# Folding the convolution taps of half the channels into TensorE products of the input projection

## The chip, the cores and the metric

The kernel runs on one core of a Trainium2 chip. The core has five engines that run their own instruction streams and meet only at semaphores: TensorE (PE, with its weight loads PEld), VectorE (DVE), ScalarE (ACT), GpSimd (POOL) and the queue that issues DMAs (SP). The metric is the device time of one execution in microseconds (us); lower is better.

## The reference

Two blocks are applied to x of shape (8, 256, 256): 8 batches, 256 time steps, 256 channels. The first is a gated state space block (Mamba), the second a linear attention with feed-forward. The change is in the front of the first, so only that is shown here:

```python
xn = _layernorm(x, ln_g, ln_b)
xn = xn * (1.0 + scale[:, None, :]) + shift[:, None, :]
xz = jnp.einsum('bsd,ed->bse', xn, in_proj_w)          # (8, 256, 1024)
x_in, z = jnp.split(xz, 2, axis=-1)                    # 512 channels each
xt = jnp.transpose(x_in, (0, 2, 1))
u = jax.lax.conv_general_dilated(xt, conv_w[:, None, :], (1,), [(D_CONV - 1, 0)],
        feature_group_count=DI, ...) + conv_b[None, :, None]   # causal, 4 taps a channel
u = jax.nn.silu(jnp.transpose(u, (0, 2, 1)))
x_dbl = jnp.einsum('bsd,ed->bse', u, x_proj_w)
dt_r, B, C = jnp.split(x_dbl, [DT_RANK, DT_RANK + N], axis=-1)
dt = jax.nn.softplus(jnp.einsum('bsr,dr->bsd', dt_r, dt_proj_w) + dt_proj_b)
# scan over time: h = h * exp(dt * A) + dt * u * B ;  y = sum over n of h * C
y = (y + u * D_param) * jax.nn.silu(z)
x = x + gate[:, None, :] * jnp.einsum('bsd,ed->bse', y, out_proj_w)
```

The convolution is depthwise: each channel d has its own four weights, and output t of channel d is the bias plus w3 x(t) + w2 x(t-1) + w1 x(t-2) + w0 x(t-3).

## The kernel before

The 512 inner channels are four blocks (`dc`) of 128 partitions. The scan over 16 states of a block is cut into four units of 4 states by 256 steps, so a batch is 16 units and the whole kernel 128 units. A unit g = 16 b + i goes through the engines like this: POOL makes the driving terms dt·u·B (line 530, `hs`, ten buffers); ACT makes the decays exp(dt·A), four activations (line 722, `ring`, two PSUM buffers); DVE scans (line 950) and multiplies by C (line 957); in four units of sixteen (i = 1, 5, 9, 13) POOL does that multiplication instead (line 539); PE sums the states by transposing adds into `sums` (lines 1293 and 1298). DVE gates a finished block with silu(z) (line 964, `ygT`).

All other work is hung into this stream at fixed places. Each engine's program is one loop over g, and tables of slots say at which g a step is issued; a step at slot -16 of batch b is issued with unit i = 0 of batch b - 1, one at slot -14 with i = 2, one at slot 19 of batch b with i = 3 of batch b + 1. So while batch b - 1 is scanned, the input projection of batch b and the attention of batch b - 2 are done between its units. Each engine works strictly through its own list.

The part that the change touches is the input projection of batch b (`in_proj`) and its convolution:

- PE, `in_proj(b, 0)` and `in_proj(b, 1)` (line 1242): two blocks of x each, four products of 128x128 weights with 256 columns. From batch 2 on all four parts of the projection use one PSUM bank, `PX`, so each has to wait until the one before has been read. `in_proj(b, 2)` and `in_proj(b, 3)` (line 1247) are z.
- ACT, `conv_last_tap(b, h)` (line 615): reads half h out of PSUM, scaled by the last tap, plus the bias, into `conv`.
- DVE, `conv_taps(b, h)` (line 916): six multiply-adds, three taps of two blocks, each reading the PSUM bank again, shifted by the tap, and adding to `conv`.
- ACT, `silu_u(b)`, then `x_proj` and `dt_proj` on PE, and so on to the next batch's decays.

Around it stand, on PE, `q_times_att` (line 1428) and `sum_states`; behind it `transpose_back` (line 1316) and `out_proj` (line 1350) of the batch before; on ACT, `decays` of unit i = 2 ahead of `conv_last_tap(b, 1)` and those of i = 3 behind it. Batch 1 is placed otherwise: both halves of x are projected in the prologue, before unit 0, into `PX` and `PY`, ahead of `setup_emb` (lines 1204 and 1187).

Of the kernel before, what the change touches and what calls it, by code (L numbers as in the profile page):

```python
# [19 lines left out]
P = 128  # L20
# [16 lines left out]
THIRDS = (0, 64, 96)  # L37
SPLIT = THIRDS[-1] + 1
ONES_ROW = RANK + 2 * N
LAST_B = NB - 1  # L40
NROW = (4 * D + NB * T) // P

# [60 lines left out]
    return None if b == 1 else b  # L103


def build(nc, a, out):
    ctx = ExitStack()
    with ctx:
        def sb(name, shape):
            return ctx.enter_context(nc.sbuf_tensor(name, shape, F32))  # L110
# [7 lines left out]
        def sem(name):  # L118
            return ctx.enter_context(nc.semaphore(name))
# [32 lines left out]
        zs = sb("zs", [P, 2, TC, DI])  # L152
        xdbl = sb("xdbl", [ONES_ROW + 1, T])
        conv = sb("conv", [P, DC, T])
        vln = conv
        dt, dtu = sb("dt", [P, 2, DC, T]), sb("dtu", [P, 2, DC, T])

# [31 lines left out]
        PZ = ps("PZ", [P, 2, T])  # L189


        staged = hs[:, 5:10].rearrange("p s n t -> p (s n t)")
        adaT = staged[:, 0:3 * KC * D].rearrange("p (k s e) -> p k s e", k=KC, s=3)
        embT = staged[:, 3 * KC * D:5 * KC * D].rearrange("p (k s e) -> p k s e", k=KC, s=2)
# [7 lines left out]
        s_ld_win = sem("ld_win")  # L202
        s_ld_w = sem("ld_w")
        s_ld_post = sem("ld_post")
        s_pool_const = sem("pool_const")
        s_sc_ready = sem("sc_ready")
        s_aexp_ready = sem("aexp_ready")
# [107 lines left out]
        def pcol(name, lo=0, hi=None):  # L315
            s, e = COLS[name]
            return par[:, s + lo:(e if hi is None else s + hi)]
# [39 lines left out]
        def _(sp):  # L357
# [23 lines left out]
            def broadcast_bc(b):  # L381

                sp.wait_ge(s_xdbl_ready, b + 1)
                sp.dma_start(bc_dram[b % 2], xdbl[RANK:RANK + 2 * N, :]).then_inc(s_bc_stored, 16)
                sp.wait_ge(s_bc_stored, 16 * (b + 1))
                if b == 0:
                    broadcast_b(b, 0)
                    for q in range(1, UPC):
                        broadcast_b(b, q)
                        broadcast_c(b, q - 1)  # L390
                    broadcast_c(b, UPC - 1)
                else:
                    for q in range(UPC):
                        broadcast_b(b, q)
                    for q in range(UPC):
                        broadcast_c(b, q)
# [11 lines left out]
            def load_seg(tile, src, seg, n, sem):  # L408
                sp.dma_start(tile, src[:, seg:seg + n].rearrange("(k p) e -> p k e", p=P)).then_inc(sem, 16)
# [14 lines left out]
            load_seg(adaT[:, :, 2], a["ada_wT"], 2 * D, D, s_ld_emb)  # L424
            load_seg(embT[:, :, 0], a["W_emb"], 0, D, s_ld_emb)
            load_seg(embT[:, :, 1], a["W_emb"], D, D, s_ld_emb)
            broadcast_bc(0)
            sp.dma_start(wo[:, :, :], a["out_wT"].rearrange("(k p) e -> p k e", p=P)).then_inc(s_ld_post, 16)
            for i, w in enumerate(("Wq", "Wk", "Wv", "W_out")):
# [33 lines left out]
        def _(pool):  # L463
# [87 lines left out]
            def rstd2(b):  # L551
                if b >= 1:
                    pool.wait_ge(s_yh_ready, TC * b)
                rstd(s_st2_ready, b, mv2, ve2, rs2, nb2, s_ve2_ready, s_rs2_ready, s_nbp2)

            for g in range(FIRST, LAST):
                if 0 <= g < NB * U:
                    inputs_of(g // U, g % U)
                if 0 <= g - BEHIND < NB * U and by_pool(g - BEHIND):
                    states_times_c((g - BEHIND) // U, (g - BEHIND) % U)  # L560
                for slot, step in ((-17, rstd0), (-1, softplus_0), (3, softplus_1), (26, residual), (28, rstd1),
                                   (40, rstd2)):
                    b = due(g, slot)
                    if b is not None and not (b == LAST_B and slot > 20) and not (b == LAST_B - 1 and step is rstd2):
                        step(b)
# [17 lines left out]
        def _(act):  # L583
# [25 lines left out]
            def conv_last_tap(b, h):  # L609
                act.wait_ge(s_xz_mm, 4 * b + h + 1)  # L610
                if b >= 1:
                    act.wait_ge(s_dt_sum, 2 * b - 1 + h)
                for e in range(2):
                    dc = 2 * h + e
                    nc.scalar.activation(conv[:, dc, :], xz_bank(b, h)[:, e, :], ACT.Identity, bias=pcol("conv_b", dc, dc + 1),  # L615
                                         scale=pcol("conv_w", TAPS * dc + 3, TAPS * dc + 4)).then_inc(s_conv0_ready, 1)

            def copy_z(b):
                if b == 0:
# [22 lines left out]
                nc.scalar.activation(u[:, 0, half], conv[:, half], ACT.Silu).then_inc((s_u_first, s_u_ready)[h], 1)  # L642

            def silu_u(b):
                act.wait_ge(s_tap_done, 3 * DC * (b + 1))
                if b >= 2:
                    act.wait_ge(s_uD_ready, DC * (b - 1))
                nc.scalar.activation(u[:, b % 2], conv[:, :, :], ACT.Silu).then_inc(s_u_ready, 1)
# [242 lines left out]
        def _(dve):  # L891
# [13 lines left out]
                stats(b, xg[:, b % XBUF], st0, mv0, s_st0_ready)  # L905

            def conv_taps(b, h):

                dve.wait_ge(s_conv0_ready, DC * b + 2 * h + 2)
                for s in range(1, TAPS):  # L910
                    for e in range(2):
                        dc = 2 * h + e
                        if s > 1:
                            dve.wait_ge(s_tap_done, 3 * DC * b + 6 * h + 2 * (s - 2) + e + 1)
                        w = pcol("conv_w", TAPS * dc + 3 - s, TAPS * dc + 4 - s)
                        V.scalar_tensor_tensor(conv[:, dc, s:], xz_bank(b, h)[:, e, 0:T - s], w, conv[:, dc, s:], ALU.mult,  # L916
                                               ALU.add).then_inc(s_tap_done, 1)
# [248 lines left out]
        def _(pe):  # L1166
# [42 lines left out]
            def transpose_x(b):  # L1209
# [7 lines left out]
                if b == 0:  # L1217
                    keep_on(8)

            def in_proj(b, h):  # L1220

                if h == 0:
                    pe.wait_ge(s_xn_ready, KD * (b + 1))
                if b == 0:
                    if h == 0:
                        pe.wait_ge(s_ld_win, 16)
                    if h == 2:
                        pe.wait_ge(s_ld_win2, 16)
                elif h == 0:
                    pass  # L1230
                elif b == 1:
                    if h >= 2:
                        pe.wait_ge(s_tap_done, 3 * DC * b + 6 * (h - 1))
                elif h <= 2:
                    pe.wait_ge(s_tap_done, 3 * DC * b + 6 * h)
                else:
                    pe.wait_ge(s_z_ready, 3 * b + 1)
                if h < 2:
                    for e in range(2):
                        lo = P * (2 * h + e)  # L1240
                        for k in range(KD):
                            ins = M(xz_bank(b, h)[:, e, :], win[:, k, lo:lo + P], xnT[:, k, :], start=(k == 0),  # L1242
                                    stop=(k == KD - 1))
                else:
                    c = h - 2
                    for k in range(KD):
                        ins = M(flat(xz_bank(b, h)), xnT[:, k, P * c:P * c + P], win[:, k, DI:2 * DI], start=(k == 0),  # L1247
                                stop=(k == KD - 1))
                ins.then_inc(s_xz_mm, 1)
                if b == 0 and h == 3:  # L1250
                    keep_on(12)
# [355 lines left out]
```

## Time and profile before

| | us |
|---|---|
| median of 3 runs | 570.05 (568.83 to 570.15) |
| the profiled execution, its own time | 569.01 |
| its span, first to last instruction | 567.2 |
| DVE busy in the span | 514.6 (91%) |
| POOL busy | 453.0 (80%) |
| PE busy, weight loads busy | 437.9 (77%), 361.2 (64%) |
| ACT busy | 408.6 (72%) |
| mean granted clock of TensorE | 0.901 of 2.4 GHz |

The rows further down are of four kinds. A row of the page or of the instruction groups names line, engine, operation, tiles and count, then busy us and mean ns, then the idle time before. A row of the waits says who waited for whom. A row of the timeline begins with start and duration in us and merges like instructions that follow each other; in square brackets stands how long the engine was idle before it and which instruction ended that. A product of f32 operands stands in the trace as two PE records, so four products are "x8".

### The profile page before, as it was taken

To read this page: it belongs to the slowest core of one execution; us is meant where nothing else is said; L and a number is where in the kernel's file an instruction comes from. 1 tells how busy PE (TensorE), PEld (TensorE's weight loads), DVE (VectorE), ACT (ScalarE), POOL (GpSimd) and SP (SyncE) were. 2 spreads that over 40 slices of the span, in tenths; PEclk is the share of its full clock that TensorE was granted. 3 is DMA by queue.
4 is the path that set the end of the run, shared out by engine and by line. 5 is a ranking of instruction groups with operands and counts; after the bars stand their busy time and mean duration, and the time that the engine had idled before them with its cause. 6 is when DMAs were issued, how large, how long until landed. Compare 5 with 4: busy or idle time off the path is not lost. (4 is left out here: it accounts for less than half of the span.)

```text
span 567.2 us, 7391 instructions
## 1 busy us (share of the span) xinstructions
PE 437.9 (77%) x2456; PEld 361.2 (64%) x2456; DVE 514.6 (91%) x566; ACT 408.6 (72%) x897; POOL 453.0 (80%) x318
## 2 busy tenths in 40 slices
PE   8967666769789787768688678768787777866887
PEld 7646445657676676656576667647674666755776
DVE  2479899999999999999999999999999999999753
ACT  2693677668865998578966999488966988486533
POOL 4049969989998889979998889978997989985121
PEclk8988777896789798998989898998899898779899
DMA  9294032201430044001440045011440045000001
GB/s 269 66 326 125 3 114 85 102 4 54 159 112 0 29 151 154 14 19 40 159 131 1 28 151 165 2 29 43 147 129 1 10 151 166 2 0 20 0 1 37
DMA packets 22366, 45.38 MB, mean 80 GB/s; under 512 B 3685, under 2 KB 13557, under 8 KB 22329
## 3 DMA queue, kind: packets, MB, share of 16 engines
q1 hardware_dynamic: 22328, 44.92, 24.3%
q8 instruction: 19, 0.31, 0.2%
q14 instruction: 19, 0.15, 0.1%
HBM read 42.52 MB, written 2.39 MB: 79 GB/s over the span
## 5 line engine op out<-in xcount | busy, mean ns | idle before, releaser
L530 POOL TENSOR_TENSOR hs<-dtu,Br 128x1024 f32<-128x1024 f32 x127 | 297.0, 2362 | 8.5 <-DMA Br<-bc_rows 8.5
L722 ACT ACTIVATE ring<-dt,Aneg 128x256 f32<-128x256 f32 x512 | 212.9, 465 | 72.6 <-DVE hs L957 68.7
L950 DVE TENSOR_TENSOR_SCAN ring<-ring,hs 128x1024 f32<-128x1024 f32 x97 | 221.4, 2282 | 5.8 <-ACT ring L722 5.4
L1298 PE MATMUL sums<-ident,hs 128*128 128x128 f32 x1024 | 150.7, 303 | 36.3 <-DVE hs L957 36.0
L1298 PEld LDWEIGHTS sums<-ident,hs 128*128 128x128 f32 x1024 | 134.4, 158 | 48.3 <-DVE hs L957 44.7
L957 DVE TENSOR_TENSOR hs<-ring,Cr 128x1024 f32<-128x1024 f32 x97 | 118.8, 1225 | 3.3
L539 POOL TENSOR_TENSOR hs<-hs,Cr 128x1024 f32<-128x1024 f32 x31 | 73.2, 2360 | 42.1 <-DVE hs L950 42.1
L950 DVE TENSOR_TENSOR_SCAN hs<-ring,hs 128x1024 f32<-128x1024 f32 x31 | 70.3, 2269 | 0.0
L1366 PE MATMUL PY<-wqkvo,xT 128*128 128x256 f32 x168 | 46.6, 428 | 0.0
L1293 PE MATMUL sums<-ident,uD 128*128 128x128 f32 x64 | 15.5, 333 | 35.2 <-DVE ygT L964 35.2
L1366 PEld LDWEIGHTS PY<-wqkvo,xT 128*128 128x128 f32 x168 | 37.5, 223 | 6.6
L615 ACT ACTIVATE conv<-PX,par 128x256 f32<-128x256 f32 x28 | 14.3, 560 | 35.8 <-PE PX L1242 35.6
L916 DVE SCALAR_TENSOR_TENSOR conv<-PX,par,conv 128x255 f32<-128x255 f32 (+2 forms) x84 | 33.9, 472 | 6.0 <-ACT conv L615 5.8
L1293 PEld LDWEIGHTS sums<-ident,uD 128*128 128x128 f32 x64 | 9.1, 168 | 38.2 <-DVE hs L957 37.7
L1242 PE MATMUL PX<-xnT,win 128*128 128x256 f32 x112 | 30.6, 421 | 3.6 <-ACT xnT L606 2.5
L1247 PE MATMUL PX<-win,xnT 128*128 128x512 f32 x52 | 27.1, 646 | 4.2 <-DVE conv L916 2.8
L1242 PEld LDWEIGHTS PX<-xnT,win 128*128 128x128 f32 x112 | 22.3, 209 | 8.0 <-ACT xnT L606 3.9
L1350 PE MATMUL PY<-wo,yg 128*128 128x256 f32 x112 | 25.3, 379 | 0.0
L1350 PEld LDWEIGHTS PY<-wo,yg 128*128 128x128 f32 x112 | 21.2, 190 | 5.4 <-issue 2.9
L481 POOL TENSOR_SCALAR ve<-mv 128x2 f32<-128x2 f32 x22 | 4.9, 222 | 24.2 <-DVE mv L899 22.9
L1178 PE MATMUL PZ<-ident,xh 128*128 128x128 f32 x56 | 10.1, 310 | 16.5 <-ACT xh L591 16.5
L1178 PEld LDWEIGHTS PZ<-ident,xh 128*128 128x128 f32 x56 | 7.5, 159 | 21.9 <-ACT xh L591 20.9
(218 smaller groups left out, 694.1 us busy)
## 6 DMA issues: line engine op xcount, KB each, us to landing
Br<-bc_rows SPq DMA_DIRECT2D x32, 512.0 KB, 5.1
Cr<-bc_rows SPq DMA_DIRECT2D x32, 512.0 KB, 4.2
xg<-in_x SPq DMA_DIRECT2D x8, 256.0 KB, 2.9
out<-fin SPq DMA_DIRECT2D x7, 256.0 KB, 4.2
hs<-in_ada_wT SPq DMA_DIRECT2D x3, 512.0 KB, 4.6
win<-in_in_wT SPq DMA_DIRECT2D x2, 512.0 KB, 6.1
hs<-in_W_emb SPq DMA_DIRECT2D x2, 512.0 KB
gate<-gate_rows SPq DMA_DIRECT2D x8, 128.0 KB, 3.1
```

Source lines behind the costliest of these rows:

```text
L530: nc.gpsimd.tensor_tensor(hs[:, g % DBUF], dtu[:, b % 2, dc, :].unsqueeze(1).to_broadcast([P, NQ, T]), Br[:, NQ * q:NQ * q + NQ, :], ALU.m ...
L539: nc.gpsimd.tensor_tensor(hs[:, g % DBUF], hs[:, g % DBUF], Cr[:, NQ * q:NQ * q + NQ, :], ALU.mult).then_inc(s_hc_pool, 1)
L722: ins = nc.scalar.activation(ring[:, g % 2, j, :], dt[:, b % 2, dc, :], ACT.Exp, scale=Aneg[:, c:c + 1])
L916: V.scalar_tensor_tensor(conv[:, dc, s:], xz_bank(b, h)[:, e, 0:T - s], w, conv[:, dc, s:], ALU.mult, ALU.add).then_inc(s_tap_done, 1)
L950: V.tensor_tensor_scan(driven if by_pool(g) else decays, decays, driven, 0.0, ALU.mult, ALU.add).then_inc(s_scan_done, 1)
L957: V.tensor_tensor(hs[:, g % DBUF], ring[:, g % 2], Cr[:, NQ * q:NQ * q + NQ, :], ALU.mult).then_inc(s_hc_dve, 1)
L1242: ins = M(xz_bank(b, h)[:, e, :], win[:, k, lo:lo + P], xnT[:, k, :], start=(k == 0), stop=(k == KD - 1))
L1247: ins = M(flat(xz_bank(b, h)), xnT[:, k, P * c:P * c + P], win[:, k, DI:2 * DI], start=(k == 0), stop=(k == KD - 1))
L1293: ins = M(YT[:, c, :], uD[:, dc % 2, P * c:P * c + P], ident[:, :], is_transpose=True, start=(c == 0), stop=False, skip_group_check=True)
L1298: ins = M(YT[:, c, :], hs[:, g % DBUF, j, P * c:P * c + P], ident[:, :], is_transpose=True, start=False, stop=(q == UPC - 1 and j == NQ - ...
L1350: ins = M(dst, yg[:, k, P * c:P * c + P], wo[:, k, :], start=(k == 0), stop=(k == DC - 1))
L1366: ins = M(dst, xT_of(b)[:, k, P * c:P * c + P], wqkvo[:, w, k, :], start=False, stop=(k == KD - 1), skip_group_check=True)
```

## The change

From batch 1 on, half 1 of x (blocks 2 and 3, the list `FOLDED`) is convolved inside the projection. As the convolution is linear, tap s of channel d can be put into the projection's weight column d; a product of that scaled column with the normalized input shifted by s steps adds that tap's share. So PE does, for each of the two blocks, four taps by two 128-row parts of the weights, all accumulating in one PSUM region at output columns s to 256, where two products stood before. DVE's six multiply-adds of this half go (`conv_taps` returns at once); ACT's reading stays, with scale 1.0 and the bias. Half 0, and all of batch 0, stay as they were.

The scaled columns are made once: a new DMA brings the four rows of taps, the same to all partitions (512 KB, `wrow`, in the buffer that unit 1 of the scan uses later), and POOL multiplies (`scale_taps`) three times into `wtap` and once in place in `win`, after batch 0's x has been projected and before its own normalization step for batch 1.

```diff
+FOLDED = (1,)
+FOLD_LO, FOLD_N = 2 * P * FOLDED[0], 2 * P * len(FOLDED)
+def folded(b, h):
+    return b >= 1 and h in FOLDED
+def taps_until(b, h):
+    return sum(3 * 2 for c in range(b + 1) for k in range(2) if not folded(c, k) and (c, k) <= (b, h))
...
+            sp.dma_start(wrow, a["tap_rows"][:, FOLD_LO:FOLD_LO + FOLD_N].unsqueeze(0).to_broadcast([P, TAPS, FOLD_N])).then_inc(
+                s_ld_taps, 16)
             broadcast_bc(0)
...
+            def scale_taps():
+                pool.wait_ge(s_ld_taps, 16)
+                pool.wait_ge(s_xz_mm, 2)
+                part = win[:, :, FOLD_LO:FOLD_LO + FOLD_N]
+                for s in range(1, TAPS):
+                    nc.gpsimd.tensor_tensor(wtap[:, s - 1], part, wrow[:, s, :].unsqueeze(1).to_broadcast([P, KD, FOLD_N]),
+                                            ALU.mult).then_inc(s_taps_ready, 1)
+                pool.wait_ge(s_taps_ready, TAPS - 1)
+                nc.gpsimd.tensor_tensor(part, part, wrow[:, 0, :].unsqueeze(1).to_broadcast([P, KD, FOLD_N]),
+                                        ALU.mult).then_inc(s_taps_ready, 1)
...
             for g in range(FIRST, LAST):
+                if g == -6:
+                    scale_taps()
...
             def conv_taps(b, h):
-
+                if folded(b, h):
+                    return
...
             def in_proj(b, h):
...
                 elif b == 1:
                     if h >= 2:
-                        pe.wait_ge(s_tap_done, 3 * DC * b + 6 * (h - 1))
+                        wait_x_read(b, h - 2)
                 elif h <= 2:
-                    pe.wait_ge(s_tap_done, 3 * DC * b + 6 * h)
+                    wait_x_read(b, h - 1)
...
-                if h < 2:
+                if h < 2 and folded(b, h):
+                    if b == 1:
+                        pe.wait_ge(s_taps_ready, TAPS)
+                    for e in range(2):
+                        lo = P * (2 * h + e)
+                        bank = xz_bank(b, h)
+                        for s in range(TAPS):
+                            for k in range(KD):
+                                w = wtap[:, s - 1, k, lo - FOLD_LO:lo - FOLD_LO + P] if s else win[:, k, lo:lo + P]
+                                ins = M(bank[:, e, s:T], w, xnT[:, k, 0:T - s], start=(s == 0 and k == 0),
+                                        stop=(s == TAPS - 1 and k == KD - 1), skip_group_check=True)
+                elif h < 2:
```

`wait_x_read(b, h)` waits for ACT's reading of half h and, where it is not folded, for DVE's taps of it.

On TensorE, between the attention product of the batch before (its rows `PY<-att,qT`) and the transposes of the gated states (`PZ<-ident,ygT`), the order before is this; `PX<-xnT,win` is half 1 of x:

```order
L1428 MATMUL PY<-att,qT 128x128 x4
L1293 MATMUL sums<-ident,uD 128x128 x2
L1298 MATMUL sums<-ident,hs 128x128 x8
L1242 MATMUL PX<-xnT,win 128x256 x4
L1316 MATMUL PZ<-ident,ygT 128x128 x4
L1316 MATMUL PY<-ident,ygT 128x128 x4
L1298 MATMUL sums<-ident,hs 128x128 x16
```

At the same place it is now this, with lines of the changed kernel (`wtap` are the scaled columns; the output's count falls with the shift):

```order
L1481 MATMUL PY<-att,qT 128x128 x4
L1346 MATMUL sums<-ident,uD 128x128 x2
L1351 MATMUL sums<-ident,hs 128x128 x8
L1289 MATMUL PX<-xnT,win 128x256 x2
L1289 MATMUL PX<-xnT,wtap 128x255 x2
L1289 MATMUL PX<-xnT,wtap 128x254 x2
L1289 MATMUL PX<-xnT,wtap 128x253 x2
L1289 MATMUL PX<-xnT,win 128x256 x2
L1289 MATMUL PX<-xnT,wtap 128x255 x2
L1289 MATMUL PX<-xnT,wtap 128x254 x2
L1289 MATMUL PX<-xnT,wtap 128x253 x2
L1369 MATMUL PZ<-ident,ygT 128x128 x4
```

Four products have become sixteen; nothing around them has changed place.

On VectorE, in the units i = 2 and i = 3 of each batch, the order before is this (`ring<-ring,hs` is the scan, `hs<-ring,Cr` the product with C, `st<-qe` statistics of the second block):

```order
L950 SCALAR_TENSOR_TENSOR ring<-ring,hs 128x1024
L957 TENSOR_TENSOR hs<-ring,Cr 128x1024
L916 SCALAR_TENSOR_TENSOR conv<-PX,par,conv 128x255 x2
L916 SCALAR_TENSOR_TENSOR conv<-PX,par,conv 128x254 x2
L916 SCALAR_TENSOR_TENSOR conv<-PX,par,conv 128x253 x2
L896 BN_STATS st<-qe 128x6 x2
L899 BN_AGGR mv<-st 128x2 x2
L950 SCALAR_TENSOR_TENSOR ring<-ring,hs 128x1024
```

Now the six multiply-adds are gone, and the scan of unit 3 follows the statistics:

```order
L986 SCALAR_TENSOR_TENSOR ring<-ring,hs 128x1024
L993 TENSOR_TENSOR hs<-ring,Cr 128x1024
L931 BN_STATS st<-qe 128x6 x2
L934 BN_AGGR mv<-st 128x2 x2
L986 SCALAR_TENSOR_TENSOR ring<-ring,hs 128x1024
```

On ScalarE, at the same units, the list reads as before but for its line numbers: the reading of half 1 (`conv<-PX,par`) stands between the decays of unit 2 and those of unit 3:

```order
L757 ACTIVATE ring<-dt,Aneg 128x256 x4
L736 ACTIVATE uD<-u,par 128x256
L649 ACTIVATE conv<-PX,par 128x256 x2
L757 ACTIVATE ring<-dt,Aneg 128x256 x4
L766 ACTIVATE yg<-PZ 128x512
```

Nothing moved there.

## Rows read from the trace of the kernel before

**Rows 1.** The page, busy time of the engines and of the taps.
```profile
PE 437.9 (77%) x2456; PEld 361.2 (64%) x2456; DVE 514.6 (91%) x566; ACT 408.6 (72%) x897; POOL 453.0 (80%) x318
...
L916 DVE SCALAR_TENSOR_TENSOR conv<-PX,par,conv 128x255 f32<-128x255 f32 (+2 forms) x84 | 33.9, 472 | 6.0 <-ACT conv L615 5.8
```

**Rows 2.** Waits over the whole span: in total, times, longest.
```profile
ACT conv L615 <- PE PX L1242: 35.6, 8, 6.5
...
DVE ring L950 <- ACT ring L722: 5.4, 6, 2.5
```

**Rows 3.** Timeline at batch 7's projection: start, duration, instruction, idle before.
```profile
420.60 1.16 PE L1428 MATMUL PY<-att,qT 128*128 128x128 f32 x8 [1.13 <-DVE att L1002]
...
422.69 1.89 PE L1242 MATMUL PX<-xnT,win 128*128 128x256 f32 x8
...
424.62 1.02 ACT L615 ACTIVATE conv<-PX,par 128x256 f32<-128x256 f32 x2 [5.11 <-PE PX L1242]
...
425.54 1.66 ACT L722 ACTIVATE ring<-dt,Aneg 128x256 f32<-128x256 f32 x4
425.68 1.23 DVE L957 TENSOR_TENSOR hs<-ring,Cr 128x1024 f32<-128x1024 f32 x1
426.82 2.42 DVE L916 SCALAR_TENSOR_TENSOR conv<-PX,par,conv 128x255 f32<-128x255 f32 x6
426.96 1.97 PE L1298 MATMUL sums<-ident,hs 128*128 128x128 f32 x16 [1.50 <-DVE hs L957]
...
429.16 0.75 DVE L896 BATCH_NORM_STATS2 st<-qe 128x6 f32<-128x256 f32 x2
...
430.11 2.27 DVE L950 TENSOR_TENSOR_SCAN ring<-ring,hs 128x1024 f32<-128x1024 f32 x1
431.12 3.62 PE L1350 MATMUL PY<-wo,yg 128*128 128x256 f32 x16
...
434.57 1.04 PE L1298 MATMUL sums<-ident,hs 128*128 128x128 f32 x8
...
437.01 0.41 DVE L964 TENSOR_TENSOR ygT<-sums,zs 128x256 f32<-128x256 f32 x1
```

**Rows 4.** Timeline, decays and scan of unit 3 during the projections of batches 2 and 3.
```profile
109.92 1.66 ACT L722 ACTIVATE ring<-dt,Aneg 128x256 f32<-128x256 f32 x4
...
113.18 2.29 DVE L950 TENSOR_TENSOR_SCAN ring<-ring,hs 128x1024 f32<-128x1024 f32 x1
...
173.31 1.66 ACT L722 ACTIVATE ring<-dt,Aneg 128x256 f32<-128x256 f32 x4
...
176.73 2.27 DVE L950 TENSOR_TENSOR_SCAN ring<-ring,hs 128x1024 f32<-128x1024 f32 x1
```

**Rows 5.** Windows: length, then busy (count) by engine, PEclk, DMA share, GB/s.
```profile
18.00:22.00 4.00, 4.00 (x16) 2.57 (x15) 2.69 (x7) 2.30 (x5) 0.00 (x0) 1.00 0.00 0
...
105.30:109.00 3.70, 3.66 (x10) 2.85 (x11) 3.70 (x2) 0.00 (x0) 3.70 (x2) 0.54 0.00 0
```

**Rows 6.** Timeline of the prologue and the first units, batch 1's projection among them.
```profile
25.18 0.22 POOL L481 TENSOR_SCALAR ve<-mv 128x2 f32<-128x2 f32 x1 [17.42 <-DVE mv L899]
...
39.72 2.36 PE L1242 MATMUL PY<-xnT,win 128*128 128x256 f32 x8
...
44.69 1.27 POOL L504 TENSOR_TENSOR dtu<-dt,u 128x512 f32<-128x512 f32 x1
...
47.85 5.16 PE L1298 MATMUL sums<-ident,hs 128*128 128x128 f32 x32
...
56.25 0.41 DVE L964 TENSOR_TENSOR ygT<-sums,zs 128x256 f32<-128x256 f32 x1
...
58.78 2.40 DVE L916 SCALAR_TENSOR_TENSOR conv<-PY,par,conv 128x255 f32<-128x255 f32 x6
...
61.54 0.60 ACT L624 ACTIVATE zs<-PX 128x512 f32<-128x512 f32 x1 [9.62 <-PE PX L1247]
...
63.73 2.30 DVE L950 TENSOR_TENSOR_SCAN ring<-ring,hs 128x1024 f32<-128x1024 f32 x1 [2.54 <-ACT ring L722]
```

More of the change, by code:

```diff
@@ L154, in build @@
         conv = sb("conv", [P, DC, T])
+        wtap = sb("wtap", [P, TAPS - 1, KD, FOLD_N])
         vln = conv
@@ L189, in build @@
         PZ = ps("PZ", [P, 2, T])
+        wrow = hs[:, 1:1 + len(FOLDED)].rearrange("p s n t -> p (s n t)").rearrange("p (s e) -> p s e", s=TAPS)
         staged = hs[:, 5:10].rearrange("p s n t -> p (s n t)")
@@ L204, in build @@
         s_ld_post = sem("ld_post")
+        s_ld_taps = sem("ld_taps")
+        s_taps_ready = sem("taps_ready")
         s_pool_const = sem("pool_const")
@@ L554, in rstd2 @@
                 rstd(s_st2_ready, b, mv2, ve2, rs2, nb2, s_ve2_ready, s_rs2_ready, s_nbp2)
+            def scale_taps():
[8 more added lines that the diff above has]
+                                        ALU.mult).then_inc(s_taps_ready, 1)
+                pool.wait_ge(s_taps_ready, TAPS)
             for g in range(FIRST, LAST):
+                if g == -6:
+                    scale_taps()
                 if 0 <= g < NB * U:
@@ L614, in conv_last_tap @@
                     dc = 2 * h + e
+                    tap = 1.0 if folded(b, h) else pcol("conv_w", TAPS * dc + 3, TAPS * dc + 4)
                     nc.scalar.activation(conv[:, dc, :], xz_bank(b, h)[:, e, :], ACT.Identity, bias=pcol("conv_b", dc, dc + 1),
-                                         scale=pcol("conv_w", TAPS * dc + 3, TAPS * dc + 4)).then_inc(s_conv0_ready, 1)
+                                         scale=tap).then_inc(s_conv0_ready, 1)
             def copy_z(b):
@@ L644, in silu_u @@
             def silu_u(b):
-                act.wait_ge(s_tap_done, 3 * DC * (b + 1))
+                act.wait_ge(s_conv0_ready, DC * (b + 1))
+                act.wait_ge(s_tap_done, taps_until(b, 1))
                 if b >= 2:
@@ L913, in conv_taps @@
                         if s > 1:
-                            dve.wait_ge(s_tap_done, 3 * DC * b + 6 * h + 2 * (s - 2) + e + 1)
+                            dve.wait_ge(s_tap_done, taps_until(b, h) - 6 + 2 * (s - 2) + e + 1)
                         w = pcol("conv_w", TAPS * dc + 3 - s, TAPS * dc + 4 - s)
@@ L1218, in transpose_x, with wait_x_read @@
                     keep_on(8)
+            def wait_x_read(b, h):
+                pe.wait_ge(s_conv0_ready, DC * b + 2 * h + 2)
+                if not folded(b, h):
+                    pe.wait_ge(s_tap_done, taps_until(b, h))
             def in_proj(b, h):
@@ L1595 @@
         "ada_b": L0_cond_ada_b, "in_wT": np.asarray(L0_cond_in_proj_w).T, "xp_wT": np.asarray(L0_cond_x_proj_w).T,
+        "tap_rows": np.asarray(L0_cond_conv_w).reshape(DI, TAPS).T[::-1],
         "dt_wT": np.asarray(L0_cond_dt_proj_w).T, "dt_b": L0_cond_dt_proj_b, "out_wT": np.asarray(L0_cond_out_proj_w).T, "Wq": L1_cond_Wq,
```

## The prediction

> **What bounds the kernel now.** I read the page first, then the waits, then the timeline around one projection, and last the same place in the other batches and in the prologue. The page says that DVE is busy for 514.6 of 567.2 us, and that the taps are 472 ns each [rows 1]. So DVE is the engine whose time is the kernel's, and what it waited for is the second question: in the whole span it waited for ACT's decays only 5.4 us [rows 2]. ACT in turn waited 35.6 us, in 8 pieces, for PE's projection of x [rows 2]. That wait costs nothing today; the timeline of batch 7 shows how near it is to costing.
>
> The reader is to follow one line there [rows 3]. PE does the attention product from 420.60, having waited for DVE's head blocks, then the sums of unit 0, then half 1 of x from 422.69, which lasts 1.89 us. Only then, at 424.62, after 5.11 us of waiting, ACT reads it; behind that, at 425.54, it makes the decays of unit 3, which end at 427.20. DVE in the meantime multiplies unit 2 until 426.91, does the six taps, 2.42 us, and the statistics of the second block, and starts the scan of unit 3 at 430.11. So the decays of unit 3 are ready 2.91 us ahead of the scan, and 2.42 us of that lead is the taps' own time.
>
> **The change part by part.**
>
> *DVE's taps.* Six fewer in each of seven batches: 7 x 2.42 = 16.9 us of DVE's time, by the stretch in which six follow each other [rows 3]. (By 472 ns each it would be 19.8 us, but neighbours overlap a little; the stretch is what DVE advances by.) They are on the path today. They pay only if the scan behind them can start earlier.
>
> *PE's products.* Twelve more per batch, 24 PE records. The price of one record in a long run: 16 of them take 3.62 us and 8 take 1.89 us, so 8 more cost 1.73 us, 0.216 each [rows 3]; the shifted ones have one to three columns fewer of 256, some 1%. 24 records are 5.1 us at the full clock. At the half clock it would be double: the window over the same eight records in batch 2 shows a granted clock of 0.54 and PE busy for 3.66 us [rows 5]. The two ends per batch are thus 5.1 and 10.3 us; I take 5.1, because in batch 7 and its like these records ran at full rate, and keep the half clock for the range. In seven batches that is 36 us of PE time; PE at 77% could carry it [rows 1], but the question is where it lies.
>
> *Where it lies.* ACT's list is unchanged: the reading of half 1 stands ahead of the decays of unit 3. Half 1 cannot start earlier either, since the sums of unit 0 and the attention product, which waits for DVE, stand ahead of it. So in batch 7: products end at 424.58 + 5.1 = 429.7, reading from 429.7, decays 0.92 us later for 1.66 us, ready at 427.2 + 5.1 = 432.3. DVE, without taps, has done unit 2 at 426.91 and the statistics 0.95 us later (429.16 to 430.11), at 427.9 [rows 3]. It then stands idle for 4.4 us, and scans unit 3 at 432.3 in place of 430.11: 2.2 us later than before. The taps were the cover of PE's product, and the edit removes the cover and lengthens what was covered.
>
> The rule for any batch: lateness = 5.1 - (scan start - end of decays). Batches 4 and 6 repeat batch 7's distances within 0.1 us, so 2.2 each. In batch 2 the decays end at 111.58 and the scan starts at 113.18: lead 1.60, lateness 3.5. In batch 3, 174.97 and 176.73: lead 1.76, lateness 3.3 [rows 4]; batch 5 repeats batch 3. Sum over batches 2 to 7: 3.5 + 3.3 + 2.2 + 3.3 + 2.2 + 2.2 = 16.7 us.
>
> *What is late next.* Behind the long product PE still has the transposes back, the sums of units 1 and 2, z, `out_proj`, and the sum of unit 3, for which DVE's gating of block 0 waits. Today DVE gets to that gating 6.9 us after the scan of unit 3 starts (430.11 to 437.01) [rows 3]. From the product's end PE needs, without a wait, some 1.2 + 1.9 + 1.8 + 3.5 + 1.0 = 9.4 us (starts and durations of the same stretch), and the scan starts 2.6 us after that end: 6.8 us. It just fits. I put 0.2 us a batch on it, 1 us in all; at half clock somewhere there it would be up to 3. DVE cannot win the lost time back elsewhere, as it hardly waits elsewhere.
>
> *Batch 1.* Its half 1 goes into `PY` in the prologue [rows 6]. PE has no idle time between it (39.72) and the sums of units 0 to 3 (47.85 to 53.0), so these end 5.1 us later, at 58.1. DVE reaches the gating of block 0 at 56.25: 1.8 us late. Then it saves 2.40 us of taps (58.78). But the next scan was already waiting 2.54 us for the decays behind ACT's copy of z, which had waited 9.62 us for PE; that z product follows a sum that waits for the late gating. So the saving falls into a wait, and the scan at 63.73 moves by between 0 and 2 us. POOL's driving term of unit 5 waits for `setup_emb` and is 4 us later, at 55.1 against its scan at 56.58: still hidden. I take +1 us.
>
> *POOL's scaling and the DMA.* Four multiplications of 128x512, by the row of that size 1.27 us each, 5.1 us [rows 6]. They can start when batch 0's x is projected, near 20 us, in a 17.42 us wait of POOL that ends at 25.18 [rows 6], so they end as it does: 0, at most 0.5 us. The 512 KB join a queue that has drained in the window from 18 to 22 us, DMA share 0.00 [rows 5], and find those engines idle. If it came late all the same, it would delay batch 1's normalization: 0 to 2 us, I take 0.
>
> *Waits.* `silu_u` and `in_proj(b, 2)` now wait for ACT's reading, which is ahead of DVE's taps in time: 0.
>
> Sum: 16.7 + 1 + 1 = 18.7 us on the profiled execution's 569.01, thus 587.7; that execution is 1.04 us under the median of 570.05. The forecast lies between, at 588 us.
>
> A word on a rule that speaks for the change. The Trainium skill, Perfetto Trace Analysis, "Identifying the Most-Contended Engine", says to take the engine with the highest occupancy and optimize it first. That engine is DVE here, and by that rule alone the time would fall by about the taps' time, to the first rival below.
>
> **The rivals.**
>
> *A, DVE's time is what counts:* the taps go and PE's products are hidden. For it: DVE's 91%, and PE's share of only 77%. Against it: the unchanged lists and the lead of 1.6 to 2.9 us that 5.1 us must fit in. It would be so if the added products ran in under half of their priced time. Time: 569 - 17 = 552 us. This is the faster one; it decides from a product that is lengthened by less than lead minus 2.42 in every batch, that is by about zero to 0.5 us, and it fades to nothing at the lead itself. Chance 0.04.
>
> *B, the clock:* the long product falls into half-clock stretches in each batch. For it: batch 2's 0.54, and the overall mean of 0.90. Against it: most projections ran at full rate, and a longer product gives PE less idle time. With half of each product at half clock, 1.7 us more for eight records, six batches add 10 us: 598. With all 32 records at half clock, 6.8 more per batch, 629. Chance for 596 and more: 0.11.
>
> The Trainium skill, TensorE: Matmul & The Clock Gate, "What's actually happening", says that activity releases the throttle. By that rule the leads of batches 2, 3 and 5 would become those of batch 7: 6 x 2.2 + 1 + 1 = 15 us, 584; it lies inside my range.
>
> *C, a cheaper product:* the shifted products overlap better than the run of 16 that I priced, or DVE's head blocks come earlier so that the chain starts earlier, and each batch loses only about the half. 3 us of 5.1 would give a lateness of 0.1 to 1.4 and 572 to 577. Chance 0.08. At exactly no change (within 0.3%, 1.7 us, about what can be told from noise here): 0.02, between A and C.
>
> *Forecast:* 0.75, from 579 to 596.
>
> **How the numbers follow.** Own range 579 to 596 holds 0.75; adding B's first step to 600 and C's upper part to 577 holds a little over 0.8. Slower by over 0.3%: forecast, B and C, 0.94. Same: 0.02. Faster: A, 0.04.
>
> **What would show it.** In the profile after: half 1's product as 32 records in about 7 us; ACT's wait for PE before its reading of half 1 grown from 5.1 to about 10 us per batch; a new DVE wait for `ring`, some 4 to 6 us, once in each of batches 2 to 7, about 28 us in total where 5.4 stood; DVE's busy time down by 17 to 20 us and the span up by 17 to 20; POOL's scaling between 20 and 25 us with batch 1's normalization not moved. If DVE's wait for `ring` stays below 10 us, the forecast is wrong and A is right; if the product lasts over 9 us in most batches, B; if it lasts under 6, C.

## The result, and the profile after

The changed kernel takes 586.34 us (median of 4 runs, 584.57 to 586.80), the kernel before 569.73 beside it: a ratio of 1.0288, 95% interval 1.0263 to 1.0313. It is 2.9% slower; the forecast was 588 us. The profiled execution took 586.24 us with a span of 584.5, which is 17.3 more than before. The page of the kernel after, to be held against [rows 1]:

```profile
PE 468.7 (80%) x2624; PEld 394.2 (67%) x2624; DVE 500.0 (86%) x524; ACT 407.1 (70%) x897; POOL 458.1 (78%) x322
...
L952 DVE SCALAR_TENSOR_TENSOR conv<-PX,par,conv 128x255 f32<-128x255 f32 (+2 forms) x48 | 19.4, 472 | 5.7 <-ACT conv L649 5.7
```

DVE works 14.6 us less, and the span is 17.3 us longer. So DVE must wait some 32 us more than it did. The waits, answering to [rows 2], say where (total, times, longest):

```profile
ACT conv L649 <- PE PX L1289: 62.0, 6, 13.2
...
DVE ring L986 <- ACT ring L757: 34.4, 11, 7.3
...
DVE ygT L1000 <- PE sums L1351: 3.2, 2, 1.9
```

DVE's wait for ACT's decays has grown by 29.0 us, and its wait for the sums stood at 1.2 before and is 2.0 longer now. With the busy time that makes -14.6 + 29.0 + 2.0 = 16.4 of the 17.3 us. A new wait of 1.8 us for `setup_emb`, shown below with batch 1, makes 18.2, and the small waits, 0.9 less in all, close the ledger. Nearly all of it is one wait. The timeline of batch 7's projection, answering to [rows 3]:

```profile
435.86 1.16 PE L1481 MATMUL PY<-att,qT 128*128 128x128 f32 x8 [1.13 <-DVE att L1038]
...
437.95 1.03 PE L1289 MATMUL PX<-xnT,win 128*128 128x256 f32 x4
...
438.62 2.28 DVE L986 TENSOR_TENSOR_SCAN ring<-ring,hs 128x1024 f32<-128x1024 f32 x1
438.81 2.73 PE L1289 MATMUL PX<-xnT,wtap 128*128 128x255 f32 x12
440.93 1.23 DVE L993 TENSOR_TENSOR hs<-ring,Cr 128x1024 f32<-128x1024 f32 x1
441.38 1.03 PE L1289 MATMUL PX<-xnT,win 128*128 128x256 f32 x4
442.07 0.74 DVE L931 BATCH_NORM_STATS2 st<-qe 128x6 f32<-128x256 f32 x2
442.25 2.73 PE L1289 MATMUL PX<-xnT,wtap 128*128 128x255 f32 x12
442.85 0.25 DVE L934 BATCH_NORM_AGGREGATE mv<-st 128x2 f32<-128x6 f32 x2
445.02 0.84 ACT L649 ACTIVATE conv<-PX,par 128x256 f32<-128x256 f32 x2 [10.25 <-PE PX L1289]
...
445.75 1.67 ACT L757 ACTIVATE ring<-dt,Aneg 128x256 f32<-128x256 f32 x4
...
447.45 2.30 DVE L986 TENSOR_TENSOR_SCAN ring<-ring,hs 128x1024 f32<-128x1024 f32 x1 [4.35 <-ACT ring L757]
```

The reader is to follow it from top to bottom. Half 1 of x is now 4 + 12 + 4 + 12 = 32 records, from 437.95 to 444.98: 7.03 us where 1.89 stood. ACT stands before it for 10.25 us, then makes the decays of unit 3. DVE is through with its statistics at 443.10 and has nothing until 447.45. Batches 4 to 7 all show this wait at 4.34 or 4.35 us. In batch 3 it is longer:

```profile
175.78 1.91 PE L1289 MATMUL PX<-xnT,win 128*128 128x256 f32 x4
...
177.49 2.90 PE L1289 MATMUL PX<-xnT,wtap 128*128 128x255 f32 x12
...
183.86 0.84 ACT L649 ACTIVATE conv<-PX,par 128x256 f32<-128x256 f32 x2 [13.18 <-PE PX L1289]
...
186.29 2.30 DVE L986 TENSOR_TENSOR_SCAN ring<-ring,hs 128x1024 f32<-128x1024 f32 x1 [7.27 <-ACT ring L757]
```

There the first records run at half speed (granted clock 0.50 from 175.78 to 177.49), 1.91 us for four instead of 1.03, and the product lasts 8.0 us. That is one of the 2.9 us by which ACT waits longer than in batch 7; the others are lost just ahead of the product, where the attention product and the sums of unit 0 run at the half clock too (the sums take 1.91 us for eight records, 1.04 in batch 7 of the kernel before).

Batch 1, answering to [rows 6]:

```profile
20.40 3.73 POOL L580 TENSOR_TENSOR wtap<-win,hs 128x512 f32<-128x512 f32 x3 [12.65 <-PE PY L1295]
24.21 1.27 POOL L583 TENSOR_TENSOR win<-win,hs 128x512 f32<-128x512 f32 x1
...
25.57 0.22 POOL L499 TENSOR_SCALAR ve<-mv 128x2 f32<-128x2 f32 x1
...
54.30 0.41 DVE L1093 TENSOR_TENSOR gate<-PZ,gb 8x256 f32<-8x256 f32 x1 [1.84 <-PE PZ L1223]
...
60.12 0.42 DVE L1000 TENSOR_TENSOR ygT<-sums,zs 128x256 f32<-128x256 f32 x1 [1.94 <-PE sums L1351]
...
61.81 1.88 PE L1300 MATMUL PX<-win,xnT 128*128 128x512 f32 x4
...
63.73 0.60 ACT L658 ACTIVATE zs<-PX 128x512 f32<-128x512 f32 x1 [11.90 <-PE PX L1300]
...
65.91 2.30 DVE L986 TENSOR_TENSOR_SCAN ring<-ring,hs 128x1024 f32<-128x1024 f32 x1 [3.17 <-ACT ring L757]
```

The scaling is done at 25.48, and POOL's next step starts 0.39 us later than before (25.18). DVE waits twice where it did not wait before: 1.84 us for the product of `setup_emb`, which `gate` reads, and 1.94 us for the late sums. So the gating of block 0 stands at 60.12, 3.87 us later than before. ACT's copy of z is only 2.19 us later, and the scan that stood at 63.73 stands at 65.91. The rows of the kernel before show why the lateness shrinks:

```profile
52.47 0.40 DVE L1057 TENSOR_TENSOR gate<-PZ,gb 8x256 f32<-8x256 f32 x1
...
58.10 3.40 PE L1247 MATMUL PX<-win,xnT 128*128 128x512 f32 x4
```

The z product took 3.40 us there, at a granted clock of 0.55, and takes 1.88 us now, at 1.00.

### The profile page after: what moved, and what is told of

It reads as the page before. It is cut to its first block and busy times, and to the rows that moved or that the text cites. A ratio compares the mean times of both kernels' runs of the same rounds, so it can differ in the third digit from the quotient of the medians.

```text
span 584.5 us, 7699 instructions
## 1 busy us (share of the span) xinstructions
PE 468.7 (80%) x2624; PEld 394.2 (67%) x2624; DVE 500.0 (86%) x524; ACT 407.1 (70%) x897; POOL 458.1 (78%) x322
## 3 DMA queue, kind: packets, MB, share of 16 engines
HBM read 43.05 MB, written 2.39 MB: 78 GB/s over the span
## 5 line engine op out<-in xcount | busy, mean ns | idle before, releaser
L986 DVE TENSOR_TENSOR_SCAN ring<-ring,hs 128x1024 f32<-128x1024 f32 x97 | 221.5, 2284 | 34.8 <-ACT ring L757 34.4
L1351 PE MATMUL sums<-ident,hs 128*128 128x128 f32 x1024 | 153.9, 308 | 30.3 <-DVE hs L993 30.2
L1351 PEld LDWEIGHTS sums<-ident,hs 128*128 128x128 f32 x1024 | 137.7, 161 | 40.6 <-DVE hs L993 37.3
L1289 PE MATMUL PX<-xnT,wtap 128*128 128x255 f32 (+2 forms) x144 | 33.0, 379 | 0.0
L1289 PEld LDWEIGHTS PX<-xnT,wtap 128*128 128x128 f32 x144 | 27.7, 192 | 3.7
L1300 PE MATMUL PX<-win,xnT 128*128 128x512 f32 x52 | 24.5, 593 | 0.0
L952 DVE SCALAR_TENSOR_TENSOR conv<-PX,par,conv 128x255 f32<-128x255 f32 (+2 forms) x48 | 19.4, 472 | 5.7 <-ACT conv L649 5.7
L519 POOL TENSOR_TENSOR dt<-dt,conv 128x512 f32<-128x512 f32 x15 | 19.2, 1277 | 1.5 <-DVE dt L974 1.0
```

The source lines that it names most:

```text
L986: V.tensor_tensor_scan(driven if by_pool(g) else decays, decays, driven, 0.0, ALU.mult, ALU.add).then_inc(s_scan_done, 1)
L1289: ins = M(bank[:, e, s:T], w, xnT[:, k, 0:T - s], start=(s == 0 and k == 0), stop=(s == TAPS - 1 and k == KD - 1), skip_group_check=True)
L1351: ins = M(YT[:, c, :], hs[:, g % DBUF, j, P * c:P * c + P], ident[:, :], is_transpose=True, start=False, stop=(q == UPC - 1 and j == NQ - ...
```

## The experiments

The theory: DVE's six taps covered PE's product; the twelve added products stand in front of ACT's reading of half 1, which stands in front of the decays of unit 3, so what counts is where they lie. The rivals: more PE time costs wherever it is put, or the costs and savings simply add up. Each kernel was timed beside the kernel before on its chip; each ratio below is to that.

**e1_no_products: the added products left out.**

```diff
-                        for s in range(TAPS):
+                        for s in range(1):
...
-                                        stop=(s == TAPS - 1 and k == KD - 1), skip_group_check=True)
+                                        stop=(s == 0 and k == KD - 1), skip_group_check=True)
```

> The changed kernel with the twelve added products left out in every batch: the output lacks three taps of half 1. DVE's taps stay removed. Theory (the long product delays ACT's reading, the decays of unit 3 behind it and the scan): without it unit 3 starts earlier than in the kernel before by the smaller of 2.4 us and the old lead of the decays, 2.4 us in batches 4, 6, 7 and 1.6 to 1.8 in 2, 3, 5, some 12 to 14 us in all: 556 us, and DVE's wait for the decays falls under 10 us. Rival 'the loss is elsewhere' (the scaling on POOL, the new DMA, the prologue): it stays near 580.

Measured: 557.65 us against 569.94, ratio 0.9789 [0.9752, 0.9825]. At the same place in batch 7:

```profile
414.29 1.89 PE L1289 MATMUL PX<-xnT,win 128*128 128x256 f32 x8
...
416.22 0.84 ACT L649 ACTIVATE conv<-PX,par 128x256 f32<-128x256 f32 x2 [5.11 <-PE PX L1289]
...
419.36 2.27 DVE L986 TENSOR_TENSOR_SCAN ring<-ring,hs 128x1024 f32<-128x1024 f32 x1
```

The product is short, the scan of unit 3 waits for nothing, and DVE's wait for `ring` falls from 34.4 to 7.6 us in the span. Whatever the change brought with it besides the products (DMA, scaling, new waits) costs little: the products are the loss of 29 us, and the taps gone are worth 12.

**e2_taps_stay: the products as in the changed kernel, and DVE's taps of half 1 done as well.**

```diff
 def taps_until(b, h):
-    return sum(3 * 2 for c in range(b + 1) for k in range(2) if not folded(c, k) and (c, k) <= (b, h))
+    return sum(3 * 2 for c in range(b + 1) for k in range(2) if (c, k) <= (b, h))
...
 def conv_taps(b, h):
-                if folded(b, h):
-                    return
...
-                if not folded(b, h):
-                    pe.wait_ge(s_tap_done, taps_until(b, h))
+                pe.wait_ge(s_tap_done, taps_until(b, h))
```

> The changed kernel with DVE's six taps of half 1 done all the same in every batch (the taps are counted twice in the output): the added products alone. Theory: the taps have to follow ACT's reading, which is 5.1 us later, so unit 3 is late by 3.8 us in batches 4, 6, 7, 5.1 in 3 and 5, 4.2 in 2, plus 2 in batch 1: 569.7 + 28 = 597 us, that is 10 to 11 above the changed kernel, since a part of the taps lies in time in which DVE now waits. Rival 'DVE's time adds up': the changed kernel plus 16.9, 603 us.

Measured: 601.64 us, 1.0566 [1.0530, 1.0602]: 15.3 us more than the changed kernel, nearer to the rival's 603 than to the theory's 597. The batches one by one (start, duration, wait before) say which is right. Batch 4 and batch 7:

```profile
252.08 0.84 ACT L649 ACTIVATE conv<-PX,par 128x256 f32<-128x256 f32 x2 [10.26 <-PE PX L1286]
...
252.96 2.43 DVE L950 SCALAR_TENSOR_TENSOR conv<-PX,par,conv 128x255 f32<-128x255 f32 x6 [3.73 <-ACT conv L649]
...
458.28 0.84 ACT L649 ACTIVATE conv<-PX,par 128x256 f32<-128x256 f32 x2 [13.24 <-PE PX L1286]
...
459.15 2.43 DVE L950 SCALAR_TENSOR_TENSOR conv<-PX,par,conv 128x255 f32<-128x255 f32 x6 [6.71 <-ACT conv L649]
...
462.44 2.27 DVE L984 TENSOR_TENSOR_SCAN ring<-ring,hs 128x1024 f32<-128x1024 f32 x1
```

DVE now waits in front of its taps. From ACT's reading to the scan of unit 3 it is 4.16 us (458.28 to 462.44), against 2.43 in the changed kernel (445.02 to 447.45), where the decays fill that time anyway: the six taps cost 1.73 us a batch and not 2.42. From the scan of unit 2 to that of unit 3, batches 3, 4 and 5 are longer by 1.7 to 1.8 us than in the changed kernel, and batch 2 by 0.8; with 1.73 each for batches 6 and 7 that is 9.5 us, near the theory's 10 to 11. Against the kernel before, unit 3 of batch 4 is late by 3.8 us, as expected. The other 4.6 us are no cost of the taps: in batches 6 and 7 ACT waited 11.63 and 13.24 us for the product, where it was 10.25 in the changed kernel, because part of PE's work ran at the half clock there (0.50 from 448.65 to 451.85 in batch 7). So the expectation missed the time by the clock, and the total alone would have named the wrong theory.

**e3_read_later: ACT reads half 1 behind the decays of unit 4, no longer ahead of those of unit 3.** Nothing else moves but the copy of `yg`, by one unit.

```diff
-for slot, step in (..., (-15, conv_last_tap_0), (-14, conv_last_tap_1),
-                   ... (19, copy_yg), ...
-    late = 2 if step in (conv_last_tap_0, conv_last_tap_1) else 1 if step is modulated else 0
+for slot, step in (..., (-15, conv_last_tap_0), (-12, conv_last_tap_1),
+                   ... (20, copy_yg), ...
+    late = 2 if step is conv_last_tap_0 else 1 if step is modulated else 0
```

> The changed kernel with ACT's reading of half 1 moved from behind the decays of unit 2 to behind those of unit 4, and the copy of the gated states (yg) behind it: the decays of units 3 and 4 wait for no product. Simple theory (ACT's order is the whole cause): DVE no longer waits, 569.7 - 14 = 556 us. Fuller theory (PE's own list is late as well: the sum of unit 3 stands behind the long product, the transposes, z and the output projection, 9.4 us behind the product's end, and DVE's gating of block 0 waits for it): DVE arrives at the gating 4 us early and waits there, so nothing is won, 584 to 587 us, with DVE's wait moved from the decays to the sums.

Measured: 580.32 us, 1.0199 [1.0153, 1.0245]. The simple theory (556) is wrong. The fuller one names the wait that stands here, but the time lies 4 us under its 584 to 587. The larger part of that is batch 3: from the scan of unit 2 to the gating it is 3.6 us shorter than in the changed kernel, at a granted clock of 1.00 here; batch 2 and batches 4 to 7 are 0.7 us shorter each. The wait has moved to another row:

```profile
DVE ygT L1000 <- PE sums L1351: 23.2, 8, 3.7
...
DVE ring L986 <- ACT ring L757: 6.6, 8, 3.2
```

and the timeline of batch 7 shows what it waits for:

```profile
442.04 3.62 PE L1403 MATMUL PY<-wo,yg 128*128 128x256 f32 x16
...
445.50 1.04 PE L1351 MATMUL sums<-ident,hs 128*128 128x128 f32 x8
...
446.57 0.42 DVE L1000 TENSOR_TENSOR ygT<-sums,zs 128x256 f32<-128x256 f32 x1 [3.68 <-PE sums L1351]
```

The sum of unit 3, which DVE's gating needs, stands behind `out_proj` and everything else that the long product pushed back. It is a second list in which the same 5.1 us had no room.

**e4_read_later_sum_first: as e3, and on PE the sum of unit 3 ahead of `out_proj`.**

```diff
 for g in range(FIRST, NB * U):
-    b = due(g, 19)
-    if b is not None:
-        out_proj(b)
     if 0 <= g < NB * U and not by_pool(g):
         sum_states(g // U, g % U)
...
+    b = due(g, 19)
+    if b is not None:
+        out_proj(b)
```

> As the kernel with the later reading, and PE sums unit 3 ahead of the output projection instead of behind it (3.5 us). Fuller theory: the gating waits under 1 us, what is late next is DVE's reading of the output projection in unit 5, about 0.4 us before its old time in batches 4, 6, 7 and 0.7 after it in the others: 566 to 572 us, near the kernel before. Simple theory: 556. Rival 'PE's added time costs wherever it stands': still 586.

Measured: 564.01 us, 0.9912 [0.9881, 0.9942], 2 us under what was expected. With two changes of order and none of work the kernel went from 586.34 to 564.01. What is left in the waits between the projections is small. Of the rows here only one wait, batch 1's for its decays, is longer than 2 us:

```profile
DVE ygT L1000 <- PE sums L1351: 5.7, 6, 1.9
...
DVE x L1008 <- PE PY L1403: 5.0, 6, 0.8
...
DVE ring L986 <- ACT ring L757: 4.2, 3, 3.2
```

**e5_products_elsewhere: the kernel before, with twelve products a batch added where PE waits for DVE** (six at the end of unit 4, six at the end of unit 6, in six batches).

```diff
+                if g % U in (4, 6) and U <= g < LAST_B * U:
+                    for i in range(6):
+                        M(spare.rearrange("p c t -> p (c t)"), win[:, i % KD, 0:P], xnT[:, i % KD, :], start=False, stop=False,
+                          skip_group_check=True)
```

> The kernel before with twelve more f32 products of 256 columns on PE in each of six batches, into an unused PSUM region: six at the end of unit i = 4 and six at the end of i = 6, where PE waits for DVE today. The same load of PE that the change adds, outside the chain. Theory (only the place of the products costs): 569.7 to 573 us. Rival 'PE has no room for 5 us more a batch': near the changed kernel's loss against its twin without products, 6/7 of 28 us, some 594.

Measured: 575.50 us against 568.55, 1.0137 [1.0104, 1.0169]. As many products a batch cost 7 us there. In front of the reading they cost 29 in seven batches (e1 against the changed kernel), which is 25 for six. The rival's 594 is out, but so is the theory, by which they would cost 3 us at most: the places weren't quite free. In the profiled execution DVE's waits for the sums (4.1 us where 1.2 stood) and for `ring` (9.3 where 5.4 stood) are 6.8 us longer; two waits of the prologue, before any added product, are 2.5 us shorter, and the span is 4.7 us longer.

**e6_before_sum_first: the control to e4, the kernel before with the sum alone moved**, by the same diff.

> Control: the kernel before, with only the sum of unit 3 moved ahead of the output projection on PE. Theory: DVE's gating does not wait for that sum in the kernel before, so nothing changes, 568 to 571 us; the gain of the mended kernel (564 against 570) needs the fold. Rival 'the new order of PE is the whole gain, the fold has none': 564.

Measured: 570.21 us against 568.55, 1.0026 [1.0001, 1.0051]: no gain. The sum's new place is worth something only to a kernel with the long product. The later reading alone was not tried on the kernel before; this control covers the sum.

**e7_z_after: as e4, and z behind `out_proj`**, so that the sum comes earlier still; ACT's copy of z two units later.

```diff
...
-(-14, in_proj_2), (-13, in_proj_3)        # PE
...
-(-11, copy_z)                             # ACT
...
+(-13, in_proj_2), (-11, in_proj_3)
...
+(-9, copy_z)
...
```

> The fold with the later reading, the sum first, and z too behind the output projection (first half of z in unit 3 after it, second half in unit 5, ACT's copy of z in unit 7). Theory: the gating's and the output projection's waits, 1.9 and 0.8 us in a batch, fall to 0.2 and 0.8 or less, 1.5 to 2 us won in six batches: 553 to 557 us. What could be late instead is the second half of z before ACT's silu in unit 7, and then x_proj: if so, 560 and more.

Measured: 562.51 us against 568.55, 0.9904 [0.9878, 0.9930]; by the ratios the same as e4 (0.9912), and 5 us above what was expected. The wait of the gating is gone from batches 2 to 7, but z is copied right ahead of ACT's silus, and DVE's next scan waits for the decays behind these:

```profile
DVE ring L986 <- ACT ring L757: 9.2, 8, 3.2
...
442.44 2.30 DVE L986 TENSOR_TENSOR_SCAN ring<-ring,hs 128x1024 f32<-128x1024 f32 x1 [1.78 <-ACT ring L757]
```

**e8_z_after_from_batch_2: as e7, folded only from batch 2 on.** The four scaled taps have their own buffer, so that batch 1 finds its weights unscaled.

```diff
-    return b >= 1 and h in FOLDED
+    return b >= 2 and h in FOLDED
...
-        wtap = sb("wtap", [P, TAPS - 1, KD, FOLD_N])
+        wtap = sb("wtap", [P, TAPS, KD, FOLD_N])
...
-                                w = wtap[:, s - 1, k, lo - FOLD_LO:lo - FOLD_LO + P] if s else win[:, k, lo:lo + P]
+                                w = wtap[:, s, k, lo - FOLD_LO:lo - FOLD_LO + P]
```

> As the kernel with z behind the output projection, and folding from batch 2 on, with all four scaled taps apart from the weights: batch 1 keeps DVE's taps and PE's prologue has 5.1 us less to do. Theory: the 2.2 us that batch 1 lost are back: 2 us below its twin, 551 to 555. Rival (the prologue's delay is absorbed): the same as its twin.

Measured: 556.84 us, 0.9803 [0.9779, 0.9827]: 5.7 us below e7 on the same chip, where 2 were expected, and 2 us above the expected 551 to 555, as e7 was too high already. In the two traces the scan of unit 2 at batch 2's projection stands at 110.81 in e7 and at 105.93 here, 4.9 us earlier. Folding batch 1 was a loss by itself.

**e9_from_batch_2: the changed kernel in its own order, folded only from batch 2 on** (the diff of e8 alone).

> The changed kernel in its own order, folding from batch 2 on only: batch 1's share alone is taken back. By the trace batch 1 costs the changed kernel 2.2 us, so 584 us; if the gap of 5.7 us between the two kernels with z behind the output projection was batch 1's doing, 580 to 581.

Measured: 582.48 us against 569.07, 1.0238 [1.0210, 1.0266]. By the ratios, batch 1 had cost 0.005 of 569, some 3 us; by the medians, 3.9. The scan of unit 2 at batch 2's projection stands at 105.92, where it was at 110.79 in the changed kernel: 4.9 us, the same as between e8 and e7. In the kernel before it was at 107.40, though batch 1 is the same work there. Most of the difference is the z product of batch 1, which took 3.40 us at a clock of 0.55 in that trace and takes 1.88 us here.

**e10_z_after_from_batch_2_again: e8 once more, in 5 rounds.**

> The fastest kernel so far, run again on the same chip in more rounds for its interval: 0.978 to 0.983 of the kernel before.

Measured: 556.64 us against 569.07, 0.9807 [0.9771, 0.9842]. It is the best version, 1.9% faster than the kernel before. Its batch 7:

```profile
410.96 7.03 PE L1286 MATMUL PX<-xnT,wtap 128*128 128x256 f32 x32
...
415.21 1.67 ACT L754 ACTIVATE ring<-dt,Aneg 128x256 f32<-128x256 f32 x4 [2.37 <-DVE hs L990]
...
416.04 2.27 DVE L983 TENSOR_TENSOR_SCAN ring<-ring,hs 128x1024 f32<-128x1024 f32 x1
...
418.03 0.84 ACT L646 ACTIVATE conv<-PX,par 128x256 f32<-128x256 f32 x2 [1.15 <-PE PX L1286]
...
422.94 0.41 DVE L997 TENSOR_TENSOR ygT<-sums,zs 128x256 f32<-128x256 f32 x1
```

The product is the same 7.03 us as in the changed kernel, which lost by it. Here the decays don't stand behind it, the scan of unit 3 starts without a wait, and so does the gating. Six batches of taps are 6 x 2.42 = 14.5 us; less 1.7 us, by which DVE's wait for `ring` stands above that of before (7.1 against 5.4), that makes 12.8, and 12.4 were measured. By the ratios it stands where e1 stood, the kernel in the old order that left the added products out (0.9807 against 0.9789).

## Why the prediction was right

Its mechanism held in batches 2 to 7; what was off there were sizes. In batch 1 it missed a wait. That the sum of 18.7 us came so near to the measured 17.3 is in part luck: the lateness of unit 3 was 2.2 us too high, the gating 1 us too high, and batch 1 2.4 us too low.

*The product's length* was right: 32 records in 7.03 us, as forecast, which is 0.214 us per added record (0.216 forecast).

*The lateness of unit 3.* Step by step, from the starts of the scans of unit 2 and of unit 3 in the two traces: added between the two were 1.8 us in batch 2, 4.5 in batch 3, 2.1, 1.85, 2.1 and 2.1 in batches 4 to 7: 14.5 in sum. Forecast were 3.5, 3.3, 2.2, 3.3, 2.2, 2.2: 16.7. Batches 4, 6 and 7 came out to 0.1. The term that was mis-sized: the leads of batches 2, 3 and 5 were priced as they stood, but they were short because PE had run part of that stretch at its half clock (0.54 in [rows 5]; in batches 3 and 5 ACT's wait was 6.49 and 6.48 us where batches 4 and 7 have 5.11). In the changed kernel the products of batches 2 and 5 ran at full rate. Batch 3 went the other way: the half clock lasted into the first records of its longer product. A short lead that comes of the half clock belongs to a place in one kernel's run, not to the batch.

*Batch 1 was mis-sized*: +1 us forecast, 3.4 measured (the scan of unit 2 at batch 2's projection, 107.40 to 110.79). The prediction had the gating 1.8 us late by the sums alone and the next scan between 0 and 2 us late. It had put nothing for DVE's `gate`, which waited 1.84 us for the delayed `setup_emb`, so the gating was 3.9 us late. The scan moved by only 2.2 us because z ran at the full clock, 1.5 us shorter than in the kernel before: that this lies near the forecast's 2 is luck. Against e9, whose z ran at full rate as well, the same scan is 4.1 us late (61.78 there). The rest of the 3.4 us is one small instruction of DVE, which took 1.57 us where it had taken 0.23:

```profile
70.53 9.29 POOL L548 TENSOR_TENSOR hs<-dtu,Br 128x1024 f32<-128x1024 f32 x4
...
78.29 1.57 DVE L1104 TENSOR_SCALAR m1s<-mods,par 128x8 f32<-128x8 f32 x1
```

Before, at 76.10, POOL was idle (from 73.9 to 79.3). No run was made to test the neighbour as the cause, but the other traces bear it out. The instruction took 1.30 to 1.57 us in the five in which a POOL multiplication still had over 1 us to run (the changed kernel, e2, e3, e4, e7) and 0.23 in the other seven, where POOL was idle or, in e8, 0.03 us from its end; in all five it ended 0.03 us after that multiplication.

*The gating behind the product* was to cost 0.2 us a batch. It cost nothing in batches 2 to 7: the 9.4 us of work fitted, with 0.7 us to spare in batch 7 (the sum of unit 3 ends at 453.65, the gating starts at 454.38). e3 shows how narrowly: once unit 3 wasn't late, the same chain cost up to 3.7 us a batch. The prediction had this as "what is late next", but only as long as the first wait stood.

*DVE's wait for `ring`* was forecast at 28 us and came to 34.4. In batches 2 to 7 it is 28.7 (4.1 in batch 2, 7.3 in batch 3, 4.3 or 4.4 in the others); 3.2 are batch 1's. *DVE's busy time* fell by 14.6, not by 17 to 20: the taps of batches 2 to 7 took 14.5 out of their group (33.9 to 19.4), those of batch 1 some 2.4, and the stretched instruction put 1.3 back; for the last 1 us no row is named here.

*The scaling and the DMA* cost 0.39 us at POOL's next step, inside the 0 to 0.5. *The rivals:* A failed by the wait of 34.4 us; B's half clock showed in batch 3 alone of batches 2 to 7, whose wait was 7.27 us where batches 4 to 7 have 4.35; C is out by the 7.03 us, and by the attention product ahead, which waits the same 1.13 us for DVE as before.

The prediction set the rule of the Trainium skill (Perfetto Trace Analysis, "Identifying the Most-Contended Engine") beside the sum. This case's trace goes against it as a forecast: the engine with the highest occupancy was relieved, from 91% to 86%, and the time rose by 2.9%; only with the lists reordered (e10) did the relief gain 1.9%. The Trainium skill's rule that activity releases the throttle (TensorE: Matmul & The Clock Gate, "What's actually happening") gave 584 us. The trace agrees with that sum in batches 2 and 5, whose products ran at full rate, and not in batch 3, where the half clock reached into the longer product. It doesn't contradict the rule itself: the granted clock rose to full at 177.82 while PE was at work.

## What to carry to other kernels

Before work is moved from the busiest engine to an idle one, look at what the removed work lay beside: if it covered a wait, read the lead (here 2.91 us, 2.42 of them the work itself) and compare it with what is added in front of the same reader. Here the added work wasn't too much for an engine with 20% to spare (e10); it stood in the wrong place in an in-order list. When the first wait is removed, expect the same microseconds at the next reader of the same engine (here `out_proj` and the sum behind it), and move both: three changes of order and one batch left out turned +2.9% into -1.9%.

## What the runs showed of the hardware

- ACT reads two PSUM blocks of 128x256 in 0.84 us where the scale is the constant 1.0 (445.02 above), and in 1.02 us where it is a column of one value per partition, as before [rows 3] and still in half 0 of the changed kernel. It gave 0.18 us a batch back.
- DVE's multiplication of 128x8 values in SBUF took 1.57 us beside a POOL multiplication and 0.23 us with POOL idle. In e2, e3 and e4 the next of its kind, which met the next POOL multiplication, took 2.39 us in place of 0.22 as well. Each of these eight long ones ended 0.03 us after POOL's instruction. A DVE instruction that is cheap by its size isn't so at every place.
- Where the clock was at its half level differed between kernels: around this product it was in batches 2, 3 and 5 before, in batch 3 in the changed kernel, and in batches 3, 6 and 7 in e2, though its mean over the span was 0.90 in all three. It moved a batch by up to 3 us, more than some of the effects in question.
